# Setting up an attention block: first pair's work reordered, vectors in one load, shift copied inside SBUF

## The reference

```
q = layer_norm(x) @ q_w;  k, v = layer_norm(context) @ kv_w
attn = where(mask, -max, q k^T / 4);  out = softmax(attn) v
x = x + out @ proj_w + proj_b
x = x + gelu(layer_norm(x) @ fc1_w + fc1_b) @ fc2_w + fc2_b
```

## Time and profile before

| | us |
|---|---|
| median of 3 runs (804.95 to 808.24) | 805.91 |
| span of the profiled execution (its own time is only given as this span) | 804.3 |
| TensorE matmuls busy | 759.1 (94%) |
| VectorE busy | 618.3 (77%) |
| ScalarE busy | 562.3 (70%) |
| POOL busy | 180.2 (22%) |

### The profile page before, as it was taken

The page is one execution under the profiler, slowest core; times in us unless marked ns, Lnnn a source line. Parts: engine busy times, 40 slices in busy tenths (PEclk is TensorE's granted clock), DMA queues, the critical chain, the costliest instruction groups (busy, mean ns, idle before and its releaser), DMA issues.

```text
span 804.3 us, 16998 instructions
## 1 busy us (share of the span) xinstructions
PE 759.1 (94%) x5615; PEld 638.3 (79%) x5615; DVE 618.3 (77%) x1379; ACT 562.3 (70%) x781; POOL 180.2 (22%) x185
## 2 busy tenths in 40 slices
PE   6748899999999999999999999999999999999998
PEld 6635779788787978878787978878797887878687
DVE  5736778798787879878887988888787888877453
ACT  4607776777777677777777778767777777776832
POOL 2311122221202222220322222021222213031230
PEclk9759999999999999999999999999999999999999
DMA  8766649385775939486594939667493956739100
GB/s 239 153 100 154 85 148 151 109 136 125 140 116 148 134 111 144 112 156 109 145 125 141 131 93 164 114 152 110 145 145 110 141 121 135 111 115 142 32 28 26
DMA packets 89478, 100.47 MB, mean 125 GB/s; under 512 B 9060, under 2 KB 63576, under 8 KB 89432
## 3 DMA queue, kind: packets, MB, share of 16 engines
q1 hardware_dynamic: 88694, 99.55, 64.7%
q10 hardware_dynamic: 754, 0.53, 0.3%
HBM read 69.22 MB, written 30.83 MB: 124 GB/s over the span
## 4 chain that ended last, share of the span: by engine, by line
PE 44%; issue 21%; DVE 13%; DMA 10%; ACT 4%; POOL 4%; SPq 2%; ACTq 1%; DVEq 0%; POOLq 0%
PE A L866 15%; PE F L866 10%; DMA QR<-qd 4%; PE F L990 3%; PE F L992 3%; PE F L991 3%; PE ST L918 2%; DMA kd<-k_lo 2%; DVE xT_hi L638 2%; DVE g_lo L594 2%; DMA qd<-q_lo 2%; DVE o_tok L680 2%; DMA xin<-in_x 1%; POOL oT_lo L434 1%; PE A L961 1%
## 5 line engine op out<-in xcount | busy, mean ns | idle before, releaser
L508 ACT ACTIVATE probs<-ST 78x512 f32<-78x512 f32 x256 | 137.5, 588 | 61.7 <-PE ST L936 58.1
L990 PE MATMUL F<-w_hi,g_hi 128*128 128x256 f32 x480 | 138.7, 289 | 0.0
L594 DVE TENSOR_TENSOR g_lo<-g_f,g_hi 128x512 fp32r<-128x512 f32 x128 | 109.3, 854 | 32.9 <-ACT g_hi L542 30.0
L992 PE MATMUL F<-w_hi,g_lo 128*128 128x256 f32 x480 | 134.0, 279 | 0.0
L991 PE MATMUL F<-w_lo,g_hi 128*128 128x256 f32 x480 | 134.0, 279 | 0.0
L528 ACT ACTIVATE QM<-mask_u 77x2048 fp32r<-77x2048 uint8 x64 | 116.8, 1897 | 0.0
L423 POOL TENSOR_TENSOR xin<-xin,projb 128x1024 f32<-128x1024 f32 x16 | 38.2, 2387 | 316.3 <-DMA xin<-in_x 316.3
L936 PE MATMUL ST<-QM,KM 127*78 127x256 f32 x512 | 94.5, 296 | 3.7 <-ACT probs L508 2.0
L990 PEld LDWEIGHTS F<-w_hi,g_hi 128*128 128x128 f32 x480 | 90.4, 188 | 6.2 <-issue 6.2
L434 POOL TENSOR_TENSOR oT_lo<-g_f,oT_hi 128x512 fp32r<-128x512 f32 x32 | 41.2, 1286 | 229.2 <-ACT oT_hi L515 229.2
L991 PEld LDWEIGHTS F<-w_lo,g_hi 128*128 128x128 f32 x480 | 90.6, 189 | 0.0
(11 more groups left out here) (168 smaller groups left out, 1891.0 us busy)
## 6 DMA issues: line engine op xcount, KB each, us to landing
QM<-qd SPq DMA_DIRECT2D x48, 512.0 KB, 14.5
xa<-in_x SPq DMA_DIRECT2D x16, 512.0 KB, 4.0
qd<-q_hi SPq DMA_DIRECT2D x32, 256.0 KB, 2.2
qd<-q_lo SPq DMA_DIRECT2D x32, 256.0 KB, 2.3
xin<-in_x SPq DMA_DIRECT2D x16, 512.0 KB, 5.0
QR<-qd SPq DMA_DIRECT2D x16, 480.0 KB, 5.2
out<-xin SPq DMA_DIRECT2D x30, 256.0 KB, 6.8
KM<-kd SPq DMA_DIRECT2D x48, 156.0 KB, 6.9
```

Source lines behind the costliest of these rows:

```text
L508: act.activation(probs[:, quad % NSLOT, 2 * (p % 2):2 * (p % 2) + 2], ST[p % 2][0:MX].rearrange("p (h n) -> p h n", n=N), ACT.Exp, scale=S ...
L594: return dve.tensor_tensor(dst, src, hi.bitcast(F32), ALU.subtract)
L990: pe.matmul(dst, g_hi[:, k, tok], w2_hi[:, k], start=(k == 0), stop=False)
L992: last = pe.matmul(dst, g_lo[:, k, tok], w2_hi[:, k], start=False, stop=(k == HC - 1))
```

## The change

The shift goes from `shiftT` to `QM` in one copy, without DRAM, so the flag is written 16 times per token (32 shift rows of 4 tiles each). The vectors come laid out as columns from the host in one load, proj_w in one load. On POOL the constants that the first statistics need come first, pair 0's rstd is computed in two parts, and the rest of the constants follows. VectorE fills `spare` in the memory of `o_tok` for TensorE's first warm-ups. High parts of pair 0's cT and xT move from VectorE to ScalarE, the score pattern is cast in two halves, the mask for the maxima comes first, the mask for the scores ahead of the proj and MLP weights, whose fc2 part stands behind the shift. VectorE's proj and MLP low parts stand behind the maxima and the normalising of pair 1. SP holds pair 1's mask and pair 0's residual load back until the shift has landed. The core of the diff:

```diff
         def spread_shift(eng, j):
             eng.wait_ge(shiftT_done, j + 1)
-            eng.dma_start(sd, shiftT.bitcast(F32)).then_inc(shift_stored, 16)
-            eng.wait_ge(shift_stored, 16 * (j + 1))
-            eng.dma_start(QM[SHIFT:ALIVE]..., sd[0:H * TT].unsqueeze(0)).then_inc(shift_loaded, 16)
-            eng.dma_start(QM[ALIVE:SROWS]..., sd[H * TT:]...to_broadcast([1, H, TT, P])).then_inc(shift_loaded, 16)
+            eng.dma_start(QM[SHIFT:SROWS].bitcast(F32).rearrange("o h (t p) -> o (h t) p", p=P),
+                          shiftT.bitcast(F32)).then_inc(shift_loaded, 16)
...
             load_ctx(0)
+            load_mask(0)
             load_xa(0)
             (kv_w, q_w)
-            load_mask(0)
             (fc1_w, fc2_w)
-            (proj_w in eight copies)
             load_ctx(1)
             load_xa(1)
+            sp.dma_start(raw_p[:], proj_rows).then_inc(pw_loaded, 16)
+            (projb, fc2b)
             store_k(0); store_q(0, 0); store_q(0, 1); gather_q_for_maxima(0)
+            sp.wait_ge(pat_done, 3)
             gather_k_for_scores(sp, 0); gather_q_for_scores(0)
+            sp.wait_ge(shift_loaded, 16)
             load_mask(1); load_xin(0, 0)
...
         ScalarE:
+            act.dma_start(columns[:], vec_columns).then_inc(vecs_loaded, 16)
+            act.wait_ge(first_consts, 1)
+            act.activation(warm[:], eps[:, 0:1], ACT.Exp)
-            act.activation(KM[:]..., pat_m[0:SROWS]...)
             mask_for_maxima(0)
+            qkv_weights_high()
+            score_patterns(slice(0, H // 2))
+            first_cT_high(); first_xT_high(1); first_xT_high(0)
             act.wait_ge(setup_done, 2 + 1)
+            act.wait_ge(consts, CONSTS)
             k_high(0)
+            score_patterns(slice(H // 2, H))
             q_high(0, 0); q_high(0, 1)
-            act.wait_ge(pat_done, 2)
+            act.wait_ge(pat_done, 3)
             gather_k_for_maxima(act, 0)
+            mask_for_scores(0)
             proj_weight_high()
-            for n in range(8):
+            for n in range(4):
                 mlp_weight_high(n)
-            mask_for_scores(0)
             shift_rows(0)
             spread_shift(act, 0)
+            for n in range(4, 8):
+                mlp_weight_high(n)
...
             def cT_split(j):
-                dve.wait_ge(shift_stored, 16 * j)
+                dve.wait_ge(shift_loaded, 16 * j)
             def shifts(j):
-                dve.tensor_scalar(shift[:, H], shift[:, 0], GONE, None, ALU.is_gt)
+                dve.tensor_scalar(shift[:, H:], shift[:, 0:1].to_broadcast([P, H, TT]), GONE, None, ALU.is_gt)
         VectorE:
-            dve.wait_ge(consts, CONSTS)
+            dve.memset(spare, 1.0).then_inc(spare_done, 1)
+            dve.wait_ge(first_consts, 2)
+            (statistics and moments of ctx, then of x; ctx normalised)
             normalise_x(0)
+            bias copy; column sums of cT; kvw_lo x2; cT_lo; xT_lo(1); qw_lo x2; xT_lo(0)
+            dve.wait_ge(consts, CONSTS)
+            k_low(0)
+            dve.wait_ge(patterns, 6)
             bv_in x2; KR pattern; q_low(0, 0); q_low(0, 1); bv; v_values(0)
+            fc1_bias_evacuate()
             ln_stats(1)
             ln_moments(1)
-            proj_weight_low(); mlp_weight_low(0..3); fc1_bias_evacuate()
             row_max(0, 0..11)
             shifts(0)
             normalise_ctx(1)
             normalise_x(1)
+            proj_weight_low(); mlp_weight_low(0..3)
...
         TensorE:
+            def keep_warm_on_spare(n):
+                for _ in range(n):
+                    pe.matmul(A[0][:, 0:256], spare[:, 512:], spare[:, 0:256], start=True, stop=True)
-            pe.wait_ge(consts, CONSTS)
-            (4 ident matmuls, transpose of vec_rows, 5 ident matmuls)
-            pe.wait_ge(vecs_done, 2)
+            pe.wait_ge(spare_done, 1)
+            keep_warm_on_spare(9)
+            pe.wait_ge(vecs_loaded, 16)
             pe.wait_ge(qkv_loaded, 2 * 16)
             bias_columns(ST[1], raw_q, 1, 0, G); bias_columns(ST[1], raw_kv, 3, G, G)
+            keep_warm_on_spare(2)
+            pe.wait_ge(first_consts, 5)
             cT(0)
+            keep_warm_on_spare(2)
             xT(0, 1)
             xT(0, 0)
+            keep_warm_on_spare(2)
...
             shift_transpose(0)
-            pe.wait_ge(setup_done, ALL_READY)
-            pe.wait_ge(shift_stored, 16)
-            keep_warm(F[0], 8)
+            pe.wait_ge(setup_done, QKV_READY + 1)
+            keep_warm(F[0], 10)
```

More of the change, by code:

```diff
@@ L401, in _, with first_rstd_ctx @@
+            pool.wait_ge(patterns, 5)
             pool.affine_select(out=pat_m[:, 0, 0:M], in_=pat_m[:, 0, 0:M], compare_op=ALU.not_equal, fill=1.0, base=-SHIFT,
-                               pattern=[[0, M]], channel_multiplier=1).then_inc(consts, 1)
-            pool.wait_ge(consts, CONSTS)
+                               pattern=[[0, M]], channel_multiplier=1).then_inc(patterns, 1)
+            def first_rstd_ctx():
+                pool.wait_ge(first_ctx_moms, NB)
+                pool.tensor_tensor(rstd[:, TT:], moms[:, TT:, 1], eps[:, TT:], ALU.add).then_inc(first_rstd, 1)
+                pool.wait_ge(first_rstd, 1)
+                pool.tensor_tensor(rstd[:, TT:], rstd[:, TT:], neg_half[:, TT:], ALU.pow).then_inc(first_rstd, 1)
@@ new lines, in first_rstd_x, with other_consts @@
+            def first_rstd_x():
+                pool.wait_ge(moms_done, TT + NB)
+                pool.tensor_tensor(rstd[:, 0:TT], moms[:, 0:TT, 1], eps[:, 0:TT], ALU.add).then_inc(rstd_step, 1)
+                pool.wait_ge(rstd_step, 1)
+                pool.tensor_tensor(rstd[:, 0:TT], rstd[:, 0:TT], neg_half[:, 0:TT], ALU.pow).then_inc(rstd_step, 1)
+            def other_consts():
+                pool.memset(count[:], 1.0).then_inc(consts, 1)
+                pool.memset(k_hi[:].bitcast(F32), 0.0).then_inc(consts, 1)
+                pool.memset(k_lo[:].bitcast(F32), 0.0).then_inc(consts, 1)
+                pool.memset(V[:], 1.0).then_inc(consts, 1)
+                pool.wait_ge(consts, 4)
+                pool.memset(count[:, :, M:MX], float(M)).then_inc(consts, 1)
+                pool.affine_select(out=V[:].rearrange("p b h e -> p (b h e)"), in_=V[:].rearrange("p b h e -> p (b h e)"),
+                                   compare_op=ALU.not_equal, fill=float(M), base=-M,
+                                   pattern=[[0, NB * H * E]], channel_multiplier=1).then_inc(consts, 1)
+                pool.wait_ge(consts, CONSTS)
@@ L760, in _, with first_cT_low, first_xT_low @@
-            normalise_x(0)
+                dve.tensor_tensor(bias[:, 2 * G:], F[0][:, 2 * G:2 * G + HC], fc1b, ALU.add).then_inc(setup_done, 1)
+            def first_cT_low():
+                dve.wait_ge(cT_hi_done, 1)
+                low(cT_lo[:], cT_cols, cT_hi[:]).then_inc(cT_lo_done, 1)
+            def first_xT_low(k):
+                dve.wait_ge(xT_hi_done, KC - k)
+                low(xT_lo[:, k], XT[k][:], xT_hi[:, k]).then_inc(xT_lo_done, 1)
+            dve.memset(spare, 1.0).then_inc(spare_done, 1)
@@ new lines, in _ @@
+            dve.wait_ge(first_consts, 2)
+            dve.wait_ge(ctx_loaded, 16)
+            for b in range(NB):
+                dve.bn_stats(stats[0:M, TT + b], cn[:, b]).then_inc(stats_done, 1)
+            dve.wait_ge(stats_done, NB)
+            for b in range(NB):
+                dve.bn_aggr(moms[0:M, TT + b], stats[0:M, TT + b]).then_inc(first_ctx_moms, 1)
+            dve.wait_ge(xa_loaded, 16)
+            for t in range(TT):
+                dve.bn_stats(stats[:, t], xa[:, t]).then_inc(stats_done, 1)
@@ new lines, in _ @@
+            dve.wait_ge(stats_done, TT + NB)
+            for t in range(TT):
+                last = dve.bn_aggr(moms[:, t], stats[:, t])
+                last.then_inc(moms_done, 1 if t < TT - 1 else 1 + NB)
+            dve.wait_ge(first_rstd, 2)
+            for b in range(NB):
+                dve.tensor_scalar(cn[:, b], cn[:, b], moms[0:M, TT + b, 0:1], rstd[0:M, TT + b:TT + b + 1],
+                                  ALU.subtract, ALU.mult).then_inc(cn_done, 1)
+            normalise_x(0)
@@ L761, in _ @@
+            dve.wait_ge(bias_mm, 1)
+            dve.tensor_copy(bias[:, 0:2 * G], ST[1][:, 0:2 * G]).then_inc(setup_done, 1)
+            per_batch = cT_cols.rearrange("p k (b m) -> p (k b) m", m=MX)
+            dve.wait_ge(cT_mm, 1)
+            dve.tensor_reduce(per_batch[:, :, M:MX], per_batch[:, :, 0:M], X, ALU.add).then_inc(c_sum_done, 1)
             for k in range(KC):
                 weight_low(kvw_lo[:, k], raw_kv[:, k], kvw_hi[:, k], 2, k, k + 1)
-            dve.wait_ge(bias_mm, 1)
@@ L790, in _ @@
             normalise_x(1)
+            proj_weight_low()
+            for n in range(4):
+                mlp_weight_low(n)
             def body(j, par, mlp, prep, ahead):
@@ L1186 @@
     arrays, args = {}, []
-    for name in _INS:
-        a = _np.asarray(inputs[name])
```

(13 more changed lines are left out.)

145 lines of the change are left out of this document (63 added, 82 removed).

## The result

The changed kernel takes 826.74 us (median of 4 runs, 821.15 to 827.87) against 806.0 us for the kernel before. The ratio, taken over all runs, is 1.0233, with a 95% interval of 1.0204 to 1.0263. The forecast was 799.5 us, so the kernel became slower where it was to become faster. The set-up became shorter by more than forecast, and the pairs gave back three times as much.

A forecast was written before the change was run, and what follows sets the result against it. TensorE was taken to bound the pairs (busy 45.5 of 46.1 us), with idle time in the set-up. Span 804.3 - 3.5 - 4.9 + 2.0 = 797.9 us, 6.4 less; off the median 799.5 us, range 794.5 to 805.

The forecast's parts named there:

- Part 1: Set-up up to the issue of the maxima's gather: 3.5 us earlier, bounds 0 and 5.3.
- t: Time in the set-up when the maxima's gather is issued, 29.46 us in the kernel before.
- Part 2: Set-up from t to the first scores: scores at t+24.2 instead of t+29.1, 4.9 us gained.
- rival B: Set-up: the shift does not queue behind the q gather, scores start 3 us earlier, 796.5 us; chance 0.15.
- Part 3: Pair 0: 2.0 us lost to the lower clock and VectorE's later cT split, bounds 0 and 4.
- Part 4: Every pair: the shift copy takes 4.1 of 6.56 us free before the scores, so nothing lost or gained.
- Rival C: Every pair: the shift copy comes 1.6 us late for the scores, 24 us over 15 pairs, 823 us; chance 0.08.
- A: Set-up: the clock stays low, t unchanged, 803.0 us; chance 0.17.
- D: Pair 0: 4 us lost as pair 1's gathers hang on its q, 801.5 us, 805 with A; chance 0.08.

The follow-up runs named there:

- e6: e5 with POOL's large set-up memsets held until the first normalise is done; 795.9 us, ratio 0.9871.
- e5: e1 with 28 instead of 10 warm-up matmuls between the first shift's transpose and the transposes of pair 1; 797.87 us, ratio 0.9878.
- e1: The changed kernel with one wait more: POOL's add of proj_b to the residual waits for the last high cast of GELU; 800.57 us, ratio 0.9917.
- e7: The changed kernel with the load of xin moved behind the next pair's context load on SP, no wait added; 800.48 us, ratio 0.9923.
- e3: The changed kernel with the shift copied inside SBUF as two copies of one row each; 832.12 us, ratio 1.0293.
- e8: The kernel before with the load of xin issued between the shift's store and the wait for it; 875.06 us, ratio 1.0841.
- e4: The kernel before with only the shift's way changed to the single copy inside SBUF, set-up as before; 824.95 us, ratio 1.0242.

## Why the prediction was wrong

- **Part 1, t: right in mechanism, the number partly by luck.** 3.5 us forecast, 3.4 measured, and the clock is up for the q projections, as given. But errors cancel: low q is done at 21.94 instead of 26.44, 4.5 us sooner, and 1.1 us is lost behind it, where the last store of q is issued 0.6 us after low q is done and takes 3.5 us to land (0.03 and 3.0 before). That stretch was taken as fixed, and so was the normalise of x, which cost 1.8 us more; e6 gives that back. Over seven kernels with nearly one set-up t lies between 23.83 and 28.22, so an agreement within 0.1 us is chance.
- **Part 2, the stretch behind t: right within 1 us.** Scores at t+23.4, forecast t+24.2. The copy queued behind the q gather, against rival B: no packet of it before 44, three from 44 to 45. The Trainium skill ("DMA: Bandwidth & Descriptors", "Queues, rings and completion order") has each DMA engine alternate between the issuers' queues; neither trace shows that. The same page's rule on the number of engines ("Why a DMA increments its semaphore by 16 and not by 1"), which the prediction cites, would put the two-row copy on two of sixteen, 12.5%; the us shown above has 15.2%, near that.
- **Part 3, pair 0: right in kind, too small.** 2.0 us were charged with bounds of 0 and 4, and 4.9 came. The stretch at the lower clock was longer than the one charged (6.8 us from 49 to 56) and two more of 3.4 us followed, at 73 and 83; e5 shows 3.2 us to be the price of TensorE's idle time ahead of the scores. The fall at 83 isn't in e1 and e7, whose pair 0 lasts 49.8; what brought it wasn't followed.
- **Part 4, every pair: this step failed**, at "Nothing is lost or gained". The copy itself was costed well enough: it lands before the scores and TensorE doesn't wait for it (4.1 us forecast of 6.56 free; in pair 0 its semaphore's last update comes 5.4 us after the issue, 1.1 us ahead of the scores). What wasn't followed was the instruction behind it on SP. Without the wait for the store the load of xin is issued 1.8 us sooner against the scores, POOL's add starts 0.8 us sooner, and the add lands on VectorE's high cast. The working did this for the set-up, where the load is held back, and not for the pairs, where it is released. Its cost, 24 us, is larger than all the rest together.
- **Rival C** had the sign and nearly the size (823) with a mechanism that is refuted: the changed kernel, e1, e3 and e7 keep the shift's copies inside SBUF, and TensorE waits for none of them in a pair. That the figure comes near is chance.
- **Rivals A and D**: the clock was up, so A fell; D's place, pair 0, lost its 4.9 us by the clock (e5) and not by the gathers, for which TensorE waits 0.6 us there and 1.4 before.

The kernel before already showed what was needed: POOL's next add runs from 107.26 to 109.65, and the low part of g beside it takes 1.91 us where it takes 0.69 elsewhere. The prediction never set the two engines' rows side by side.

```profile
108.30 1.91 DVE L594 TENSOR_TENSOR g_lo<-g_f,g_hi 128x512 fp32r<-128x512 f32 x1
```

## What to carry to other kernels

When a wait is taken out of a queue, list what stands behind it in that queue and follow each item to the engine that it wakes, since a transfer that comes sooner can cost more than one that comes late. Where VectorE and POOL both work on SBUF, write down the start times of their instructions side by side: here an add of POOL that began first held VectorE's cast until it ended. An edge that keeps POOL behind the critical cast cost nothing here, since POOL has idle time, and makes the time independent of a race of hundredths of a microsecond.

## What the runs showed of the hardware

- **Some instructions of VectorE and POOL exclude each other.** A cast of 0.43 us lasts 2.35 to 2.65 beside an add that began first, and ends 0.28 to 0.29 us after it (194.65 and 194.37). A lead of 0.02 us is enough. The same holds for VectorE's difference of two tensors in SBUF (0.69 to 2.69 in e8), and for a normalise beside memsets (1.38 to 3.20). The Trainium skill ("SBUF — State Buffer", "Who interferes with whom") says this: a port pair shared by the two engines is taken for a whole instruction by whoever issues first, and the other is blocked. It also lets VectorE's instructions with at most one input from SBUF and outside its faster modes go free, and the traces agree: those that read PSUM kept their 0.48 and 0.68 us beside the second add (from 194.33 to 196.88 in the long pair).
- **A short stall can cost about as much again.** In five of the ten long pairs, after waits of 1.1 to 1.2 us (in some with a second one of 0.3 to 0.6), TensorE's granted clock was at the lower level for 3.4 us, by the two levels an estimated 1.7 us of a busy TensorE. The other five had such waits and no fall; in e1, without the waits, it never fell in these pairs. What decides wasn't found.
- **The race shows in the spread of the times.** e4's runs reach from 817.81 to 829.78 us, the kernel before on the same chip from 805.27 to 810.61 (thirteen runs); with the add behind the cast (e1) four runs lie between 798.62 and 801.35.
- **The copy's packets.** 512-byte packets onto two partitions: 38 in one us for 15.2% of sixteen engines' time, 64 ns each, and 53 in another for 13.9%, 42 ns. The forecast had 47.
- **A copy on few DMA engines delays the load behind it.** Beside the single copy, POOL's add follows the issue of xin by 5.9 us (94.08 to 99.95), beside two copies of one row (e3) by 4.4 (94.62 to 99.03). In the changed kernel thirteen of the load's sixteen semaphore updates are in by 97.42 and the last two come at 99.72 and 99.88; from 97.5 to 99.5 its packets take 15.4% and 11.3% of the sixteen engines' time, about two engines. In e3 all sixteen come between 98.58 and 98.97. That fits two engines that had the copy to do first and start late on their share of xin; which engine moved which packet isn't in the trace.
